# A decoder block on one core: from chunks of 512 tokens to chunks of 256, in three threads beside one endless scan

## The reference

```
x = _layernorm(x + _L0_attn_ref(x, ...))      # a Mamba block: rmsnorm, in_proj to 2 x 512 channels, causal conv of 4 taps,
                                              # silu, x_proj to dt (16), B (16), C (16), delta = softplus(...), then
    s = s * dA + dBu                          # the selective scan: 512 channels x 16 states, one step per token,
    y = jnp.einsum('bds,bs->bd', s, C_t)      # with dA = exp(delta * A) and dBu = delta * B_t * u_t
    # y = (y + u * D) * silu(z);  out_proj;  + x
x = _layernorm(x + _L0_xattn_ref(x, ctx, ctx, ...))  # 8 heads against 128 keys made of the context twice, rotary q and k,
                                              # out projection, + x, layer norm, linear, relu
x = _layernorm(x + _L0_ffn_ref(x, ...))       # 8 experts of 256 x 256 (w1, w3, w2), all computed, the top 2 weighted in,
                                              # plus a shared expert
```

## Time and profile before

| | us |
|---|---|
| median of 3 runs (1152.98 to 1157.36) | 1153.48 |
| the profiled execution, whole time | 1155.19 |
| its span in the profile | 1153.4 |

### The profile page before, as it was taken

One profiled execution on the slowest core, in us unless ns is written; L12 is line 12 of the kernel. 1 busy time (PEld: TensorE's weight loads), 2 busy tenths in 40 slices (PEclk: granted clock), 3 DMA queues, 4 the chain that ended last, 5 costly groups with the idle time before them and its releaser, 6 DMA issues.

```text
span 1153.4 us, 12464 instructions
## 1 busy us (share of the span) xinstructions
PE 894.8 (78%) x3960; PEld 681.1 (59%) x3960; DVE 812.2 (70%) x1254; ACT 490.4 (43%) x929; POOL 475.0 (41%) x280
## 2 busy tenths in 40 slices
PE   4845557948769999577779999387799974867996
PEld 2434345336558885266568884275578862645885
DVE  1699997579999956588989964698989751213232
ACT  3535552745445525544445417454444321312222
POOL 1257980174446720553637510743547313000231
PEclk9955558878779999787789999795799996755998
DMA  6115731100315421212026412102044412001452
GB/s 205 38 73 175 247 124 38 56 36 20 110 51 170 152 96 55 74 37 92 19 75 199 138 56 92 55 19 91 19 147 151 148 41 109 1 0 34 157 169 70
DMA packets 42895, 104.95 MB, mean 91 GB/s; under 512 B 4432, under 2 KB 12761, under 8 KB 42831
## 3 DMA queue, kind: packets, MB, share of 16 engines
q1 hardware_dynamic: 42830, 104.16, 27.5%
HBM read 88.21 MB, written 11.74 MB: 87 GB/s over the span
## 4 chain that ended last, share of the span: by engine, by line
PE 57%; DVE 17%; POOL 10%; issue 9%; ACT 5%; DVEq 0%; DMA 0%; POOLq 0%; ACTq 0%; SPq 0%
PE ps L916 17%; PE ps L993 10%; PE ps L772 8%; PE ps L851 5%; DVE hs L1099 5%; POOL dbu L561 5%; PE ps L890 3%; PE ps L879 3%; DVE yacc L1149 3%; POOL w13x L548 2%; PE ps L960 2%; DVE mx L1233 2%; PE ps L830 1%; ACT work L725 1%; PE ps L845 1%
## 5 line engine op out<-in xcount | busy, mean ns | idle before, releaser
L561 POOL TENSOR_TENSOR dbu<-v,bbc 128x1024 f32<-128x1024 f32 x128 | 304.1, 2385 | 213.3 <-DVE v L1085 112.3
L1099 DVE TENSOR_TENSOR_SCAN hs<-ps,carry,dbu 128x512 f32<-128x512 f32 x256 | 313.3, 1265 | 8.2 <-issue 8.0
L772 PE MATMUL ps<-ident,hs 128*128 128x128 f32 x1024 | 180.3, 333 | 93.8 <-DVE yacc L1149 78.9
L674 ACT ACTIVATE ps<-delta,neg_a 128x512 f32<-128x512 f32 x256 | 173.3, 691 | 171.6 <-DVE hs L1099 171.4
L772 PEld LDWEIGHTS ps<-ident,hs 128*128 128x128 f32 x1024 | 151.8, 175 | 122.5 <-DVE hs L1099 97.5
L916 PE MATMUL ps<-x_hi,w13x 128*128 128x512 f32 x576 | 175.5, 428 | 0.0
L596 POOL TENSOR_TENSOR work<-work,cbc 128x512 f32<-128x512 f32 x64 | 86.7, 1355 | 203.8 <-ACT work L760 154.3
L1149 DVE SCALAR_TENSOR_TENSOR yacc<-ps,ctok,yacc 128x512 f32<-128x512 f32 x240 | 167.2, 737 | 1.2 <-PE ps L772 1.0
L760 ACT ACTIVATE work<-ps,half_b 128x512 f32<-128x512 f32 x72 | 49.6, 689 | 211.9 <-PE ps L916 211.9
L993 PE MATMUL ps<-w2s,work 128*128 128x256 f32 x576 | 136.3, 380 | 0.3
L1255 DVE SCALAR_TENSOR_TENSOR work<-ps,vec,work 128x512 f32<-128x512 f32 x72 | 54.1, 751 | 105.6 <-PE ps L916 85.5
(11 more groups left out here) (163 smaller groups left out, 1081.1 us busy)
## 6 DMA issues: line engine op xcount, KB each, us to landing
w13x<-w_dram SPq DMA_DIRECT2D x72, 512.0 KB, 3.4
bbc<-brow_dram SPq DMA_DIRECT2D x32, 512.0 KB, 4.2
w_dram<-w13x SPq DMA_DIRECT2D x18, 512.0 KB, 2.9
w2s<-in_w SPq DMA_DIRECT2D x36, 256.0 KB, 2.7
cbc<-comb_dram SPq DMA_DIRECT2D x32, 256.0 KB, 3.9
work<-in_w SPq DMA_DIRECT2D x18, 256.0 KB, 3.5
work<-work SPq DMA_DIRECT2D x16, 256.0 KB, 2.3
xn<-in_x SPq DMA_DIRECT2D x4, 512.0 KB, 4.4
```

The lines of the kernel that those rows point to most:

```text
L561: pool.tensor_tensor(dbu[:, i % DRING, :, :], v[:, 2 * h:2 * h + 2, :], bbc[:, n // 2 % 2, n % 2, :].rearrange("p (o t) -> p o t", o=1) .t ...
L674: act.activation(ps[:, unit % 2, :], delta[:, q, :], ACT.Exp, scale=neg_a[:, q * NS + m:q * NS + m + 1]).then_inc(da_done.sem, 1)
L772: last = pe.transpose(ps[:, bank, t * P:(t + 1) * P], src(t), ident[:, :])
L1099: dve.tensor_tensor_scan(hs[:, m % 2, q, 0:TC], ps[:, unit % 2, :], dbu[:, n % DRING, q % 2, :], carry[:, m, q:q + 1], ALU.mult, ALU.add). ...
```

## The change

- `TC` is 256: eight chunks of two tiles. A piece of the scan is 256 tokens long. The unit of the scan is now a *slot*: two pieces (half the channels of one state), 32 slots per chunk, 256 in all, numbered through without a gap.
- The schedule is one list for the whole program. In each slot g stand, in this order: the sum of slot g - 3 (`LAG`), the scan of slot g, the steps of the second half of the chunk before the one that is scanned, and one step of the preparation of the *next* chunk. `u`, `sz`, `delta`, `v`, `yacc` and `ctok` have two buffers for it. The preparation has 23 steps (`R_...`) in slots 4 to 26. The second half has 24 steps up to the router (`S_YT` to `S_X2T`) in the first 14 slots (`FRONT`), and 23 for the experts in the other 18. After slot 258 the second half of the last chunk stands alone.
- An expert is two steps, both halves at once: `gate_rows` makes 24 matmuls of 256 columns (before, for 512 tokens, 24 of 512), each with its own weight load. Its weights are loaded once per chunk, so eight times in all instead of four.
- PSUM: two banks for exp (half a bank per piece), one bank for the transposed states (2), one bank for the whole preparation (3), four for the second half (4 to 7). Both tiles of the attention have banks of their own.
- Several instructions are merged over the width (silu, exp, ln, `delta`, `v` as one of 1024 elements), the softmax's scale is folded into the keys (the small L1236 is gone), and each engine's copy of `carry` now carries the reset at a sequence's start.

The core of the diff, on the schedule and on the scan of each engine:

```diff
-TC = 512
+TC = 256
...
-WRING, CRING = 2, 2
-HRING = 3
-DRING = 3
+WRING, HRING = 3, 3
+CGROUPS = 2
+DRING = 4
...
+SLOTS = 2 * NS
+LAG = 3
...
+PRE_SLOT = 4
+FRONT = 14
+
+
+def second_slot(k):
+    if k < S_MOE:
+        return k * FRONT // S_MOE
+    return FRONT + (k - S_MOE) * (SLOTS - FRONT) // (S_END + 1 - S_MOE)
 
 
 def schedule():
 
-    tick = lambda t: [("early", t), ("mid", t), ("late", t)]
-    steps = [("setup", 0), ("pre", 1), ("post", 3), ("post", 4), ("pre", 2), ("post", 5), ("pre", 3)] + tick(0)
-    steps += [("pre", 4), ("pre", 5), ("early", 1), ("pre", 6), ("late", 1), ("setup", 1)]
...
+    for g in range(slots + LAG):
+        i, s = divmod(g, SLOTS)
+        if g >= LAG:
+            steps.append(("sum", 0, g - LAG))
+        if g < slots:
+            steps.append(("scan", 0, g))
+        for j in range(CHUNKS):
+            first = SLOTS * (j + 1) + LAG
+            for k in range(S_END + 1):
+                if first + second_slot(k) == g:
+                    steps.append(("second", j, k))
+        if i + 1 < CHUNKS and 0 <= s - PRE_SLOT <= R_DELTA:
+            steps.append(("pre", i + 1, s - PRE_SLOT))
...
+    steps += [("second", CHUNKS - 1, k) for k in range(S_END + 1)]
...
+            def inputs(i):
+
+                j, s = divmod(i, SLOTS)
+                n, h = divmod(s, 2)
+                group = i // (2 * BROWS)
+                pool.wait_ge(*bbc_in[group % 2].at(0, 16 * (group // 2 + 1)))
+                pool.wait_ge(*v_done.at(j, 1))
+                pool.wait_ge(*scan_done.at(0, max(0, i - DRING + 1)))
+                pool.tensor_tensor(dbu[:, i % DRING, :, :], v2[:, j % 2, 2 * h:2 * h + 2, :],
+                                   twice(bbc[:, group % 2, n % BROWS, :]), ALU.mult).then_inc(dbu_done.sem, 1)
...
+            def state_rows(i):
+
+                n, t = divmod(i, 2)
+                pe.wait_ge(*scan_done.at(0, 2 * (n + 1)))
+                pe.wait_ge(*y_done.at(0, i))
+                transposes(ps[:, 2, :], [hs[:, n % 2, q, t * P:(t + 1) * P] for q in range(Q)]).then_inc(ht_ps.sem, 1)
...
+                if n == S_S:
+                    if j == 0:
+                        pe.wait_ge(kv_done.sem, 2)
+                    pe.wait_ge(*q_done.at(j, 2))
+                    pe.wait_ge(*res_done.at(j, 1))
+                    scores(j, 0)
+                    scores(j, 1)
...
+            def gate_rows(bank, e, s):
+
+                for ib in range(2):
+                    for i, (a, r) in enumerate(((0, x2_hi), (1, x2_hi), (0, x2_lo))):
+                        for k in range(KD):
+                            last = pe.matmul(half(bank, ib), weights(2 * e + ib, a, s, k).bitcast(F32R),
+                                             r[:, k, :].bitcast(F32R), start=(i == 0 and k == 0),
+                                             stop=(i == 2 and k == KD - 1))
+                return last
...
+            def scan(g):
+                j, s = divmod(g, SLOTS)
+                m, h = divmod(s, 2)
+                dve.wait_ge(*da_done.at(0, g + 1))
+                dve.wait_ge(*dbu_done.at(0, g + 1))
+                if h == 0 and g >= 4:
+                    dve.wait_ge(*ht_ps.at(0, g - 2))
+                    dve.wait_ge(*carry_done.at(0, g // 2 - 1))
+                for q in (2 * h, 2 * h + 1):
+                    last = dve.tensor_tensor_scan(hs[:, m % 2, q, :], half(g % 2, q % 2), dbu[:, g % DRING, q % 2, :],
+                                                  carry[:, m, q:q + 1], ALU.mult, ALU.add)
+                last.then_inc(scan_done.sem, 1)
```

More of the change, by code:

```diff
@@ L544, in mixer, with scan @@
-                if kind == "scan" and 1 <= n < 2 * NS - 1:
-                    inputs(j, n + 1)
-                if kind == "split" and n < 2 * ALL:
+            def scan(g):
+                for i in range(g + 2 if g else 0, min(g + 3, SLOTS * CHUNKS)):
+                    inputs(i)
+            def inputs(i):
[7 more added lines that the diff above has]
+                                   twice(bbc[:, group % 2, n % BROWS, :]), ALU.mult).then_inc(dbu_done.sem, 1)
@@ L607, in _ @@
+            for kind, j, n in SCHEDULE:
+                if kind == "pre":
+                    pre(j, n)
+                elif kind == "scan":
+                    scan(n)
+                elif kind == "split":
+                    split(n)
+                elif kind == "second":
+                    second(j, n)
         @block.scalar
@@ L768, in _ @@
+            act.wait_ge(consts.sem, CONSTS)
+            for kind, j, n in SCHEDULE:
+                if kind == "pre":
+                    pre(j, n)
+                elif kind == "scan":
+                    scan(n)
+                elif kind == "split":
+                    split(n)
+                elif kind == "second":
+                    second(j, n)
         @block.tensor
         def _(pe):
-            def transposes(bank, src, tiles, sig):
-                for t in range(tiles):
-                    last = pe.transpose(ps[:, bank, t * P:(t + 1) * P], src(t), ident[:, :])
-                last.then_inc(sig.sem, 1)
@@ L775, in mixer, with transposes, setup @@
-            def mixer(j, kind, n):
-                if kind == "setup" and n == 1:
+            def transposes(o, srcs):
+                for t, src in enumerate(srcs):
+                    last = pe.transpose(o[:, t * P:(t + 1) * P], src, ident[:, :])
+                return last
+            def setup(n):
+                if n == 1:
                     pe.wait_ge(w_setup.sem, 7 * 16)
@@ new lines, in _ @@
+            for kind, j, n in SCHEDULE:
+                if kind == "pre":
+                    pre(j, n)
+                elif kind == "scan":
+                    scan(n)
+                elif kind == "sum" and n >= SLOTS * CHUNKS - 2:
+                    if n == SLOTS * CHUNKS - 2:
+                        state_rows(n)
+                        state_rows(n + 1)
+                elif kind == "setup":
+                    setup(n)
+                elif kind == "second":
+                    second(j, n)
```

1450 lines of the change are left out of this document (716 added, 734 removed).

## The result

The changed kernel takes **1384.3 us** (median of 4 runs, 1374.0 to 1388.2) against 1153.2 before: ratio 1.198, 95% interval 1.191 to 1.205. Slower was forecast, 1206 us was not: the time lies 109 us above the range. The profiled execution took 1383.2 us with a span of 1381.4. Medians here are over executions in the fast state; one of four executions each of e5 and e11, over 1.5% above the fastest, is left out.

The account below looks back on a forecast made before the run. The prediction took DVE to bound attention and PE the experts. Start 55, first chunk 92, seven periods of 133 (work 107 plus waits) 931, lag 6, last second half 120 and 1.8 outside the span gave 1206 us, range 1090 to 1275.

Parts of the forecast that it names:

- DVE's work per period: VectorE's busy time per 256-token chunk, scans, split and small instructions included: from 101.2 to 107 us.
- the extra weight loads: TensorE's expert gate products: 24 loads per expert and 256 tokens hide behind the matmuls, 0 us; unhidden up to 12 per period.
- DVE's waits: Second term of a period: VectorE's waits for other engines, 21.5 us in the front plus 5 in the expert slots.
- out projection: Front of the second half: 16 TensorE instructions, 3.5 us, beside a sum and a slot's scans; VectorE waits 1.5.
- rotation and scores: Attention in the front: VectorE waits about 3 us for the rotated queries and 5.7 for the scores, 8.5 together.
- attention output: Front of the second half: VectorE waits 2 us for the attention output of two tiles.
- second norm: Front, after attention: GpSimd, ScalarE and TensorE steps of 3.5 us, less part of a slot; VectorE waits 2.
- experts and router: 18 expert slots: VectorE waits 4 us where two steps meet on TensorE, plus 1 for the router: 5.
- The first chunk: 32 slots of scans, setup, preparation of the next chunk and 11 us of waits: 92 us.
- break-even period of 125.8: Period at which the new kernel equals the old, other terms held; VectorE may then wait 19 us per period.
- the rivals on the fast side: Mainly that VectorE's waits are covered in front and experts: period 117 us, kernel 1094 us; chance 0.28.
- PE's clock falls in the front: Rival: TensorE at 1.2 GHz in the front adds about 10 us to VectorE's path: period 143, 1276 us; chance 0.15.

Follow-up runs that it names:

- e5: Changed kernel with the scan thread working on 32 columns only, all instructions, waits and transposes kept: 1242.1 us.
- e11: Changed kernel with TensorE's transposes of the scan's states moved from the start to the end of each slot: 1489.6 us.
- e3: Changed kernel plus 12 idle TensorE matmuls per chunk, 8 before the rotated queries and 4 before the feed-forward's input: 1393.9 us.
- e9: Changed kernel without the four DMAs that swap neighbouring rows of the queries: 1365.5 us.
- e15: Changed kernel with tanh for silu and logarithm in the preparation, so its four table loads per chunk are gone: 1350.6 us.
- the thin runs: Changed kernel with the scan thread on 32 columns, once with all state transposes (1242.1 us), once with one of four (1234.3 us).
- e6: Kernel before with chunks of 256 tokens and the scan thread on 32 columns only: 1253.7 us.
- e7: Kernel before, chunks of 512 tokens, with the scan thread on 32 columns only: 1032.2 us.
- e4: Kernel before with its old schedule, only the chunks cut from 512 to 256 tokens: 1325.5 us.
- e16: Kernel before with chunks of 256 and a quarter of each transfer of the experts' first weights: 1300.7 us.
- e10: Changed kernel plus only eight idle TensorE products ahead of the wait for the rotated queries: 1385.4 us.
- e13: Changed kernel with three of the four transposes of each slot's states left out on TensorE: 1374.4 us.
- e14: Changed kernel with the scan thread on 32 columns and only one of four state transposes per slot: 1234.3 us.
- e1: Changed kernel with DVE's steps of the second half's front one slot later than the other engines': 1401.1 us.
- e2: Changed kernel with the second half's front spread over 20 slots in place of 14: 1373.6 us.
- e8: Changed kernel with the preparation packed into slots 16 to 26, two steps a slot: 1451.3 us.

## Why the prediction was wrong

**What held.** Start to the first scan (56.5 for 55); DVE's work per period (109.4 for 107; the scans' share at its upper bound, 732 ns for 680: 64 of them, +3.3); the DMA of the weights, which TensorE waited for 1.7 us in all; the extra weight loads (six gate products, each with its own load, take 0.70 us in the last chunk, 24 of them 2.8 for the 2.75 forecast). The last second half took 128 for 120.

**The step that failed is the second term of the period, "DVE's waits": 26.5, measured 48.9.** By its own items in the period at 484 us: out projection 1.5, measured 3.8; the rms step 1.5, 1.1; rotation and scores 8.5, 13.2 (6.5 + 6.7); softmax to values 6, 6.2; attention output 2, 6.3; second norm 2, 4.5 (3.9 + 0.6); sums and gating behind TensorE 0, 2.7; experts and router 5, 10. Most of the excess in the front stands behind TensorE, whose products I had "at full clock". An estimate from the rows: out projection, queries, first scores, attention output and linear layer took about 12 us longer here than the same products at the full clock (5.7 for 3.5; 6.1 and 3.8 for 3.7 and 1.9 by the scores of e3, which have the queries' shape; 3.3 for 1.8 per tile by e9; 6.4 for 3.4 by e3). The linear layer had no term of its own: the 3.9 in "second norm" is the wait for it. In the experts' part 3.1 of the 10 us are the wait behind the silu block on ScalarE, for which I had nothing.

**The first chunk** missed by 14 us for another reason, and it is one of work. DVE waited 12.2 us there, for 11 forecast, but it was busy 93.5 us, for some 80. Two of its instructions ran into products of GpSimd:
```profile
136.24 6.50 DVE L1149 TENSOR_SCALAR delta<-v 128x1024 f32<-128x1024 f32 x1
605.72 0.69 DVE L1149 TENSOR_SCALAR delta<-v 128x1024 f32<-128x1024 f32 x1 [1.43 <-ACT v L676]
```
The second line is the same instruction three chunks on, with GpSimd idle. The other one (L1135 at 87.05) took 5.2 us in place of 0.2. Together that is 10.8 us.

**But the form was worse than the items.** I added work and waits, as if the waits stood and the work could be traded. e5 took 49 us of work and the period fell by 17. e9 and e15 took next to nothing from DVE and moved it. What the runs support is a period that is a length, made longer by what shares its queues:

- the second half alone, from the last chunk: front 74 + experts 47 = 121 us;
- the preparation beside it: front 89.9 against 81.8 without it in the last period, experts' part 64.5 against 52.8: 20 us. With that 141, and 3 to 4 us from L1303 to the next first sum; the thin runs show 141.1 and 140.7 (there the preparation may cost a little less);
- the scan thread: 158.4 - 141.1 = 17 us, part of it perhaps the lower clock beside it.

These three are differences between runs and stages, not parts that were each taken out alone; that they add up is in part by construction.

The second half has one chunk in flight. My own sum had its length, 120 us for the last chunk, beside a break-even period of 125.8. That left 6 us for a preparation and 32 slots of scans in the same queues; read so, the rivals on the fast side had no room. The chance of 0.28 for them was wrong on evidence I already had.

**Why shorter chunks are slower.** The length has a part that doesn't shrink with the tokens (64 us of 144, e6 and e7): by my reading small instructions, hand-overs between engines, swap, norms. Four bodies paid it before, eight do now. Without the scans this costs 221 us; with them, e4 shows 172. That these are the same loss, partly covered by scans, is argued and not shown; e16 only shows that the traffic is not its main part. Where a step is latency, DVE's share falls: 107 in 133 was forecast as 80%, 109.4 in 158.4 is 69%.

**Where the hidden preparation's gain went.** Before, it had a stage of its own, 48 us per 512 tokens. But the first 14 of them (430 to 444) are the last expert's end, the gating and the out projection, which now belong to the second half; the preparation itself, but for its first norm steps, takes some 34 to 37 us, about 18 per 256. Now it is beside two other threads and costs 20: as far as this comparison goes, nothing was hidden. It was turned into waits: about 4 us of them in ScalarE's queue (e15). In_proj's half-clock blocks in the front (3.8 us for 1.9) are another place; no run takes them out alone.

**The rivals.** The rival "PE's clock falls in the front" (143, 1276 us) was right in its mechanism: the front had 0.71, and 0.65 without preparation, and its 10 us are near the 12 estimated above. It is part of the failed step and not the whole: with it the period would be 145. It also explains spread between periods: the shortest front of the changed kernel (88.7 us) had the highest clock (0.75), the longest (91.3) the lowest (0.70). The runs meant to lift the clock gave nothing: e3 and e10 won the scores' 2.6 us and lost it beside. How much a front at full clock throughout would give wasn't reached by any run and stays open. The prediction also takes it that transposes don't count as activity for the clock. The clock of 0.50 beside nothing but transposes fits that, but e13 and e14 speak against it: with three of four transposes of the states gone, the front's clock fell from 0.71 to 0.64 and from 0.83 to 0.66. Open too is how the 7 us a period of the new order over e4 divide; e1, e2, e8 and e11 show only that this order is near the best of those tried. No version of the new order came below the kernel before, not even those that leave most of the scan out (e5, e14); of the shorter-chunk versions that leave nothing out, e4 is the nearest.

## What to carry to other kernels

Before adding work and waits, write down how long the longest serial thread takes alone; with one item in flight the period can't be under it, and a stage that exists once per chunk has a part that halving the chunk doubles. "Hidden" is a property of each in-order queue, not of idle shares: ScalarE was idle 55% of the time and taking 5 us a period from it still gave 4, because a wide function with its table loads stood ahead of two short steps that others waited for. Filler work covers a wait only if it needs none of the engines that the waiting step is queued on. And products in a stage with gaps are to be priced at the clock granted there, not at the full one.

## What the runs showed of the hardware

- A scan of 256 f32 columns takes 732 ns and one of 512 takes 1265: so 2.08 ns a column and 199 ns each; the thin ones of 32 columns took 268, which fits (66 + 199).
- DVE and GpSimd exclude each other on products of two SBUF operands. Of the 72 on L1315 (128 x 512), 44 began with GpSimd idle and took 0.66 to 0.70 us. The other 28 began during a GpSimd product, and each ended 0.55 us after that product had. A GpSimd product that began during DVE's took 1.5 to 1.75 us in place of 1.3. The mean of the line is 1011 ns; in the kernel before it was 758 (L1249).
```profile
1331.74 0.69 DVE L1315 SCALAR_TENSOR_TENSOR work<-work 128x512 f32<-128x512 f32 x1 [1.82 <-ACT work L784]
589.99 1.68 DVE L1315 SCALAR_TENSOR_TENSOR work<-work 128x512 f32<-128x512 f32 x1 [2.66 <-ACT work L784]
```
- A row of GpSimd products without a gap can hold a DVE instruction back through several of them: L1149 at 136.24 (one SBUF operand) took 6.5 us in place of 0.69, while GpSimd ran five in a row.
- A table load on ScalarE takes 1.28 us, as long as 1.2 functions of 128 x 1024.
